# Gated linear attention: the output projection is issued in the next tile's group, the RMS norm is parted around a copy, and the drain of the attentions gets wide value products

## Reference

```python
g = jnp.cumsum(gc, axis=1)
qg, kg = qc * jnp.exp(g), kc * jnp.exp(-g)
A = jnp.einsum('cthd,cshd->chts', qg, kg) * tril
o = einsum(A, v) + einsum(qg, S)      # S: state, decayed and added to
```

## Time and profile before

| | |
|---|---|
| runs | 2923.86 us median of 3 (2919.88 to 2928.68) |
| profiled execution | 2922.78 us, its span 2921.4 us |
| granted TensorE clock, mean | 0.981 |
| TensorE busy | 2735.9 us (94%) |
| VectorE busy | 2485.6 us (85%) |
| ScalarE busy | 2066.5 us (71%) |
| GpSimd busy | 920.0 us (31%) |
| value products L401 | 8192 records, 637.9 us |
| exponentials L644 | 2048, 1085.5 us |

### The profile page before, as it was taken

One profiled execution on the slowest core, in us unless ns is written; L12 is line 12 of the kernel. 1 busy time (PEld: TensorE's weight loads), 2 busy tenths in 40 slices (PEclk: granted clock), 3 DMA queues, 4 the chain that ended last, 5 costly groups with the idle time before them and its releaser, 6 DMA issues.

```text
span 2921.4 us, 58119 instructions
## 1 busy us (share of the span) xinstructions
PE 2735.9 (94%) x23131; PEld 1247.4 (43%) x23131; DVE 2485.6 (85%) x3270; ACT 2066.5 (71%) x3906; POOL 920.0 (31%) x1052
## 2 busy tenths in 40 slices
PE   8999999999999999999999999999888799888899
PEld 2222222236666622222222366665333365467655
DVE  8999999987777699999999777776898956899744
ACT  6999999986666579999999766664766524745232
POOL 1000000013454410000000134453587554299810
PEclk9999999999999999999999999999999999989999
DMA  2000000000000010000000000000000000000000
GB/s 96 6 16 17 17 17 17 17 9 1 2 2 1 2 55 11 17 16 17 15 15 15 13 1 2 1 2 28 0 1 0 10 1 1 0 1 1 1 1 15
DMA packets 29148, 33.62 MB, mean 12 GB/s; under 512 B 13195, under 2 KB 23438, under 8 KB 28622
## 3 DMA queue, kind: packets, MB, share of 16 engines
q1 hardware_dynamic: 28878, 29.92, 3.5%
HBM read 17.58 MB, written 7.34 MB: 9 GB/s over the span
## 4 chain that ended last, share of the span: by engine, by line
PE 65%; DVE 20%; ACT 8%; issue 4%; POOL 2%; DMA 0%; DVEq 0%; SPq 0%; POOLq 0%; PEldq 0%; ACTq 0%
PE banks L401 15%; PE banks L383 10%; DVE max_parts L528 7%; PE banks L376 6%; PE banks L1122 2%; PE banks L2150 2%; PE banks L2135 2%; PE banks L1097 2%; PE banks L2137 2%; ACT probs L644 2%; PE banks L1030 2%; DVE banks L3001 2%; DVE state_keys L2998 2%; PE banks L1140 2%; DVE banks L3003 2%
## 5 line engine op out<-in xcount | busy, mean ns | idle before, releaser
L528 DVE TENSOR_REDUCE max_parts<-banks 128x2 f32<-128x1024 f32 x1024 | 1170.6, 1218 | 9.5 <-PE banks L376 8.2
L644 ACT ACTIVATE probs<-banks 128x512 f32<-128x512 f32 x2048 | 1085.5, 599 | 59.1 <-PE banks L383 32.5
L383 PE MATMUL banks<-q_parts,k_parts 51*128 51x512 bf16 x2048 | 653.9, 384 | 5.1 <-ACT v_heads L603 1.5
L401 PE MATMUL banks<-probs,v_heads 128*9 128x256 f32 x8192 | 637.9, 383 | 8.2 <-ACT pv_copy L655 2.0
L376 PE MATMUL banks<-k_parts,q_parts 48*128 48x512 bf16 x2048 | 594.5, 385 | 10.3 <-DVE max_parts L528 6.0
L711 POOL CAST neg_max_parts<-neg_max 128x8 bf16<-128x8 f32 x64 | 13.0, 204 | 1120.5 <-DVE neg_max L533 1120.5
L383 PEld LDWEIGHTS banks<-q_parts,k_parts 51*128 51x128 bf16 x2048 | 151.7, 94 | 474.6 <-ACT probs L644 397.2
L401 PEld LDWEIGHTS banks<-probs,v_heads 128*9 128x9 f32 x8192 | 123.4, 88 | 382.0 <-issue 343.0
L1684 POOL TENSOR_TENSOR state_times_c<-state,c_row 128x1024 f32<-128x1024 f32 x63 | 148.1, 2355 | 90.8 <-ACT c_row L2000 55.4
L2321 ACT ACTIVATE silu_a<-banks 128x512 f32<-128x512 f32 x80 | 47.7, 597 | 163.1 <-PE banks L2135 162.9
L1878 DVE TENSOR_TENSOR_SCAN state<-banks,state_carry,state 128x512 f32<-128x512 f32 x128 | 157.3, 1271 | 6.4 <-ACT banks L1995 4.3
(11 more groups left out here) (527 smaller groups left out, 4998.1 us busy)
## 6 DMA issues: line engine op xcount, KB each, us to landing
outT_half<-pv_copy SPq DMA_DIRECT2D x248, 16.0 KB
prob_sums<-pv_copy SPq DMA_DIRECT2D x248, 2.0 KB
q_scratch<-qk_parts SPq DMA_DIRECT2D x8, 384.0 KB, 3.5
k_scratch<-qk_parts SPq DMA_DIRECT2D x8, 384.0 KB, 2.6
k_parts<-k_scratch SPq DMA_DIRECT2D x28, 96.0 KB
q_parts<-q_scratch SPq DMA_DIRECT2D x28, 96.0 KB
q_parts<-neg_max_rows SPq DMA_DIRECT2D x128, 3.0 KB
ffn_weights<-moe SPq DMA_DIRECT2D x1, 1928.0 KB, 7.8
```

The source lines that it names most:

```text
L383: nc.tensor.matmul(bank("exp", n, x)[:, :], K[p % 2][half_of(x, ROWS + PARTS), tile(t)], Q[p % 2][half_of(x, ROWS + PARTS), blk(j)], start ...
L401: i = nc.tensor.matmul(PVb[group:group + VD, cols], V[:, t + k, 2 * (s // NB) + x, :], PT[:, (n + k) % RING, x, cols], start=(t == 0 and c ...
L528: nc.vector.tensor_reduce(mxp[s % 2][:, :, u // NB, u % NB], Mb[m % 2].rearrange("p (x k) -> p x k", x=2), AX.X, ALU.max).then_inc(*maxed. ...
L644: nc.scalar.activation(PT[:, n % RING, x, :], bank("exp", n, x)[:, :], ACT.Exp, scale=float(HD) ** -0.5).then_inc(*exped.inc())
```

## The change

GLA: for t < 15 the projection of tile t is issued in tile t+1, behind `scores(t + 1, 0)` and the spread; `add_x` follows the mask of the dense scores there. `rms` is parted: Ln, then the copy of k0, then Exp, then the copy of q0. Where masks are late, their transposes and copy come ahead of those of k1, and the lists of bank uses are put in the same order. Attention: in the drain, pairs 246 to 255 have one call of `values` with 512 columns, at step 2k+4; `spread_sums` is issued ahead of `values`; the tiles of the sums and of `heads_up` have 64 rows, the added ones zero; for the last half of the last block ScalarE makes the inverse by Ln and Exp, ahead of the rotation angles; `keep_busy` goes from 4 and 6 matmuls to 3 and none.

```diff
-        sums = sb("prob_sums", [HEADS, 2, N])
+        sums = sb("prob_sums", [64, 2, N])
-        heads_up = sb("heads_up", [HEADS, HEADS, HD])
+        heads_up = sb("heads_up", [64, HEADS, HD])
...
+        narrow_pairs = (UNITS_ALL - AHEAD + 4) // 2
+        pairs_valued = lambda k: 2 * min(k, narrow_pairs) + max(0, k - narrow_pairs)
...
                 if j == LAST:
                     pe.wait_ge(evacuated, STAGES)
-                    g.keep_busy(PVb, (4, 6)[c])
+                    if c == 0:
+                        g.keep_busy(PVb, 3)
...
-                if n >= 3 and (n - 3) // 2 * 2 < UNITS_ALL:
-                    values((n - 3) // 2 * 2, (n - 3) % 2)
                 for c in range(2):
                     for j in range(LAST):
                         if n == final_at(j) + c:
                             spread_sums(j, c)
+                if n >= 3 and (n - 3) // 2 < narrow_pairs:
+                    values((n - 3) // 2 * 2, slice((n - 3) % 2 * 256, (n - 3) % 2 * 256 + 256))
+                elif n % 2 == 0 and narrow_pairs <= (n - 4) // 2 < UNITS_ALL // 2:
+                    values(n - 4, slice(0, 512))
...
-                act.wait_ge(valued, 2 * ((n - RING) // 2 + 1))
+                act.wait_ge(valued, pairs_valued((n - RING) // 2 + 1))
...
+            act.wait_ge(sums_spread, 2 * LAST + 2)
+            act.wait_ge(normalised, 2 * LAST)
+            nc.scalar.activation(inverse[:, 1, :], g.ps[1][:, 0:256], ACT.Ln).then_inc(*last_inverted.inc())
+            act.wait_ge(last_inverted, 1)
+            nc.scalar.activation(inverse[:, 1, :], inverse[:, 1, :], ACT.Exp, scale=-1.0).then_inc(*last_inverted.inc())
             if beside:
                 beside.on_act()
...
-            nc.gpsimd.memset(sums[:, :, blk(LAST)], 0.0).then_inc(*ends_zeroed.inc())
+            nc.gpsimd.memset(sums[:, :, :], 0.0).then_inc(*ends_zeroed.inc())
...
                 if t == 0:
                     gate_project(0)
                     scores(0, 1)
+                else:
+                    project(t - 1)
...
                     turn_halves(t + 1)
+                    if t in LATE_MASKS:
+                        turn_mask(ring, LATE_MASKS[t])
                     turn_k1(t + 1)
                     turn_q1(t + 1)
                 for b in LATE_TURNS[t] if t in LATE_TURNS else ():
                     turn(b)
-                if t in LATE_MASKS:
-                    turn_mask(ring, LATE_MASKS[t])
-                project(t)
+                if not after:
+                    project(t)
...
                 mask_scores(t, 0)
                 if t == 0:
                     finish_gates(1)
+                else:
+                    add_x(t - 1)
                 mask_queries(t)
...
                 square(t)
+                rms_log(t)
+                if after:
+                    copy_k0T(t + 1)
                 rms(t)
                 if after:
-                    copy_k0T(t + 1)
                     copy_q0T(t + 1)
+                if t in LATE_MASKS:
+                    copy_mask(ring, LATE_MASKS[t])
+                if after:
                     copy_k1T(t + 1)
                     copy_q1T(t + 1)
```

More of the change, by code:

```diff
@@ L277, in attention @@
         scored, maxed, joined, max_turned, max_copied, max_split, scored_T, exped, valued, evacuated = main
-        late = g.signals("sums_added sums_spread outs_spread halves_added sums_inverted normalised o_projected x_added")
-        sums_added, sums_spread, outs_spread, halves_added, sums_inverted, normalised, o_projected, x_added = late
+        late = g.signals("sums_added sums_spread outs_spread halves_added sums_inverted last_inverted normalised o_projected x_added")
+        sums_added, sums_spread, outs_spread, halves_added, sums_inverted, last_inverted, normalised, o_projected, x_added = late
         units = [(0, 0)] + [(1, b) for b in range(NB)] + [(0, b) for b in range(1, NB)]
@@ L390, in turn_max, with values @@
                                  start=True, stop=True).then_inc(*max_turned.inc())
-            def values(n, c):
+            def values(n, cols):
                 s, t = n // STAGE, n % STAGE
-                cols = slice(256 * c, 256 * c + 256)
                 pe.wait_ge(v_copied, NB)
@@ L401, in values @@
                         i = nc.tensor.matmul(PVb[group:group + VD, cols], V[:, t + k, 2 * (s // NB) + x, :], PT[:, (n + k) % RING, x, cols],
-                                             start=(t == 0 and c == 0), stop=(t == STAGE - 2), skip_group_check=True)
+                                             start=(t == 0 and cols.start == 0), stop=(t == STAGE - 2), skip_group_check=True)
                 i.then_inc(*valued.inc())
@@ L486, in on_pe @@
                             spread_sums(j, c)
+                if n >= 3 and (n - 3) // 2 < narrow_pairs:
+                    values((n - 3) // 2 * 2, slice((n - 3) % 2 * 256, (n - 3) % 2 * 256 + 256))
+                elif n % 2 == 0 and narrow_pairs <= (n - 4) // 2 < UNITS_ALL // 2:
+                    values(n - 4, slice(0, 512))
+                for c in range(2):
                     if n == final_at(LAST) - 1:
@@ L536, in add_sums @@
                 dve.wait_ge(gathered[j % 2], gathered_of(j))
-                nc.vector.tensor_tensor(sums[:, 0, blk(j)], sums[:, 0, blk(j)], sums[:, 1, blk(j)], ALU.add).then_inc(*sums_added.inc())
+                nc.vector.tensor_tensor(sums[0:HEADS, 0, blk(j)], sums[0:HEADS, 0, blk(j)], sums[0:HEADS, 1, blk(j)], ALU.add).then_inc(*sums_added.inc())
             def normalise(j, c):
-                dve.wait_ge(sums_spread, 2 * j + c + 1)
-                dve.wait_ge(normalised, 2 * (j - 1) + c + 1)
-                nc.vector.reciprocal(inverse[:, c, :], g.ps[c][:, 0:256]).then_inc(*sums_inverted.inc())
+                if j < LAST or c == 0:
+                    dve.wait_ge(sums_spread, 2 * j + c + 1)
+                    dve.wait_ge(normalised, 2 * (j - 1) + c + 1)
+                    nc.vector.reciprocal(inverse[:, c, :], g.ps[c][:, 0:256]).then_inc(*sums_inverted.inc())
                 if j < LAST:
@@ L547, in normalise @@
                 outs = oT[0][:, half_blk(j, c)] if j < LAST else g.ps[2 + c][:, 0:256]
-                dve.wait_ge(sums_inverted, 2 * j + c + 1)
+                if j < LAST or c == 0:
+                    dve.wait_ge(sums_inverted, 2 * j + c + 1)
+                else:
+                    dve.wait_ge(last_inverted, 2)
                 nc.vector.tensor_tensor(oTn[:, half_blk(j, c)], outs, inverse[:, c, :], ALU.mult).then_inc(*normalised.inc())
@@ L876, in gla_ffn @@
             if t in LATE_MASKS:
-                tile_uses = tile_uses[:-1] + [("mask", LATE_MASKS[t]), tile_uses[-1], ("same", LATE_MASKS[t])]
+                tile_uses = tile_uses[:-3] + [("mask", LATE_MASKS[t])] + tile_uses[-3:-1] + [("same", LATE_MASKS[t]), tile_uses[-1]]
             uses += tile_uses
@@ L881, in gla_ffn @@
             if t == LATE_BLOCKS:
-                uses += [(u, b) for b in range(1, NB) for u in ("glow", "low", "logit")]
+                uses = uses[:-1] + [(u, b) for b in range(1, NB) for u in ("glow", "low", "logit")] + uses[-1:]
         entry = Ring(g.ps[0:7], ENTRY_USES, readers)
@@ L1424, in on_dve @@
                     state_decay(t + 1)
-                add_x(t)
+                else:
+                    add_x(t)
                 if t == LATE_BLOCKS:
@@ L1523, in square, with rms_log, rms @@
                 nc.scalar.activation(flat(o_q), flat(o_t), ACT.Square).then_inc(*squared.inc())
-            def rms(t):
+            def rms_log(t):
                 act.wait_ge(sums_made, t + 1)
                 nc.scalar.activation(flat(o_q), bank("rs", t)[:, :], ACT.Ln, bias=g.eps_ln[:, :], scale=1.0 / DK).then_inc(*sums_log.inc())
+            def rms(t):
                 act.wait_ge(sums_log, t + 1)
```

4 lines of the change are left out of this document (1 added, 3 removed).

## The result

| | before | after |
|---|---|---|
| runs, median | 2919.84 us of 6 | 2906.36 us of 6 (2904.13 to 2908.08) |
| ratio | | 0.9941, interval 0.9928 to 0.9954 |
| profiled execution, its span | 2922.78, 2921.4 us | 2908.08, 2906.8 us |
| granted TensorE clock, mean | 0.981 | 0.979 |
| TensorE busy | 2735.9 us | 2726.4 us |

The kernel is faster, by 13.5 us between the medians; the ratio's interval says 13 to 21 us. The forecast time of 2913.5 lies 7.1 us above the measured one. It stood 10.4 us under the 2923.86 of the runs shown first; the kernel before now came out 4.0 lower, and counted from there the forecast promised 6.3 us of the 13.5.

The account below looks back on a forecast made before the run. TensorE was taken to bound the GLA tiles and the attention drain; 6.0 us from GLA plus 4.2 us from the attentions, 10.2 us off the profiled 2922.78, gave 2912.6, or 2913.5 on the median's footing; range 2904 to 2920.

Parts of the forecast that it names:

- What bounds the kernel, and which hole closes and which opens: GLA tile: TensorE bounds; the 0.46 us idle before q1's transposes closes, one of 0.45 us opens before the scores.
- Scores, spread and projection (1.33 + 1.06) then end at 879.69, against 879.85: gain 0.16 us a tile: Steady GLA tile on TensorE: scores wait for q0T until 877.30, yet the sequence ends 0.16 us earlier.
- GLA's 6.0 us: Both GLA passes: 3.0 us saved in each, from 2.1 us in the tiles and 0.9 us at the last transition.
- I take 0.15 for all of tiles 0 to 13: GLA tiles, early ones with late masks included: 0.15 us saved in each, 14 x 0.15 = 2.1 us a pass.
- The last transition, 0.9 us: GLA's tile 15: scores and masks come 1.2 us earlier, the addition to x takes 0.3 back, 0.9 us saved.
- Attention, 2.1 us each: Each attention's end: 0.6 us from wide value products in the drain, 1.5 us from an earlier second projection.
- ScalarE just free: End of first attention: rotation angles run until 654.6, next norm needs ScalarE at 654.7, so no cost.
- (a): GLA tiles: the hole before the scores vanishes, each tile gives 0.6 us, 2901 us; chance 0.14.
- (b): Hole only moved: tiles and value products give nothing, only ends of attentions and passes gain, 2919 us; chance 0.22.
- (c): GLA tiles slower: q0T's copy 0.8 us later than put, each of 28 tiles loses 0.64 us, 2935 us; chance 0.03.
- the clock (d): TensorE's clock falls to 1.2 GHz in the GLA tiles, some 550 us more, 3464 us; chance 0.01.

Follow-up runs that it names:

- q0T first: Changed kernel with ScalarE's order Ln, k0T, q0T, Exp instead of Ln, k0T, Exp, q0T: 2901.63 us, ratio 0.9936.
- the kernel with all edits: Changed kernel plus q0T before Exp, decay before normalisation, fewer keep-busy matmuls, late last projection, parted angles: 2920.58 us; with GpSimd's state decay held back 2892.54 us.

## Why the prediction was right or wrong

*What bounds the kernel, and which hole closes and which opens*: right. The parted norm brought q1's transposes to 2.48 us behind the sum of squares and q0T's copy to 2.72, both within 0.01 us of the forecast. The new hole was taken too large (0.28 us recorded, 0.45 forecast).

*"Scores, spread and projection (1.33 + 1.06) then end at 879.69, against 879.85: gain 0.16 us a tile"*: this is the step that failed, in its size: 0.41 us a tile measured, and with it GLA's 6.0 us, where 11.8 came. It took the calls' lengths from the old order, and a gain of 0.16 is a small difference of long terms. What it missed: the scores start 0.05 us after q0T's copy, not 0.1, and so 0.07 earlier; the projection lasts 0.95 instead of 1.06 between the spread and the cumulation; the cumulation's first product 0.43 instead of 0.48 behind the projection. 0.16 + 0.07 + 0.11 + 0.05 is 0.39 of the 0.41. 0.26 us more than the 0.15 taken, over ten tiles in two passes, is 5.2 of the 5.8 us by which GLA exceeded its 6.0; the rest is in the next step.

*"I take 0.15 for all of tiles 0 to 13"*: tiles 1 to 5 gave 0.22, 0.18, 0.25, 0.25, 0.6 us more than that in both passes together. These tiles were not taken apart.

*The last transition, 0.9 us*: right. It shows as 1.20 at tile 0 to 1 (there the projection leaves the path to the scores) and -0.29 in tile 15, where the projection and the addition to x of tile 14 now stand: 0.91. That VectorE and GpSimd set the end there was only half the truth: the 15 keep-busy matmuls set it, 1.7 us behind GpSimd (1004.48 against 1006.16 in the changed kernel).

*Attention, 2.1 us each*: the ends 1.59 for 1.5; the drains 0.88 and 0.53 for 0.6. *"ScalarE just free"* for the norm was right (norm's Ln at 656.82, 0.03 us after its input, the angles over at 656.71), and no further cost of table changes showed. But it cost 0.3 us in another place, since GpSimd starts its constants for GLA only when ScalarE is through, and then runs beside VectorE's norm. I had not asked who else waits for ScalarE.

*The rivals*: (a), the hole vanishing, did not happen by itself. The runs with q0T first are what it would have been, and it is worth 0.17 and not 0.45 us, for lack of cover; (b) and (c) fell; the clock (d) stayed at 1.00 in the steady tiles of every trace, and in the last tile with fewer keep-busy matmuls too, except in the first pass of the kernel with all edits, where it fell.

*The sums*: 2923.86 less 10.2 is 2913.7 and not 2913.5, and in (c) the ends and last tiles add up to 6.0 and not 6.6; neither slip changes a reading.

## What to carry to other kernels

Two edits can be worth next to nothing alone (0.10 and -0.04 us a tile) and 0.41 together; price them in the order they leave behind, and don't call a small difference of long chains a gain without giving the calls' lengths their own error. Before moving an instruction ahead of another, ask what its result releases on other engines and whether that runs into a neighbour: here the new order of two VectorE instructions cost 0.97 us a tile, and one wait on GpSimd gained 1.13. Where keep-busy matmuls stand in front of a wait, compare their end with the time at which what is waited for is done, and read the granted clock of that stretch again after every further edit, in each pass.

## What the hardware showed that was not expected

- The same TensorE call, the projection, takes 0.95, 0.99 or 1.06 us by the calls around it, to 0.01 us in every steady tile. What in the hardware makes it so, no run here tells.
- VectorE's 128x512 multiplication with both inputs in SBUF lasts 2.03 us instead of 0.69 when it starts within a GpSimd operation of 2.33 us, and ends 0.55 us behind it.
- The same idle time of 1.61 us in the last tile was followed by 3.4 us at a granted clock of 0.50 in one pass and by none in the other. And near the start of each attention, in all 16 traces, 3.4 to 20.5 us pass at 0.50.
- Two table loads of 1.28 us each were followed by the next activation 0.01 us after their end.
